# A selective-scan block on one core: softplus with two fitted factors, and five instead of four products with B per unit made by GpSimd

## The reference, cut to what matters

```
u = silu(causal_conv(in_proj(seq)))
dt, B, C = split(x_proj(u))
dt = softplus(dt_proj(dt) + bias)          # max(v, 0) + log(1 + exp(-|v|))
for each token t:
    h = exp(dt_t * A) * h + (dt_t * u_t) * B_t      # 256 channels x 16 states
    y_t = sum over states of h * C_t
out = out_proj((y + u * D) * silu(z))
```

## Time and profile before

| what | value |
|---|---|
| median of 3 runs | 1283.58 us |
| the profiled execution | 1284.42 us, its span 1282.6 us |
| instructions with a busy time | PE 3642, DVE 1341, ACT 1532, POOL 747 |
| chain that ended last, by engine | POOL 27%, DVE 24%, issue 21%, PE 19%, ACT 7% |
| mean granted TensorE clock | 0.936 of full speed |
| data moved | 116.78 MB, 90 GB/s over the span |

### The profile page before, as it was taken

One profiled execution on the slowest core, in us unless ns is written; L12 is line 12 of the kernel. 1 busy time (PEld: TensorE's weight loads), 2 busy tenths in 40 slices (PEclk: granted clock), 3 DMA queues, 4 the chain that ended last, 5 costly groups with the idle time before them and its releaser, 6 DMA issues.

```text
span 1282.6 us, 13041 instructions
## 1 busy us (share of the span) xinstructions
PE 1072.5 (84%) x3642; PEld 613.6 (48%) x3642; DVE 1150.1 (90%) x1341; ACT 819.0 (64%) x1532; POOL 1106.9 (86%) x747
## 2 busy tenths in 40 slices
PE   5678878888888887888888889888878878888797
PEld 4334545545545544544455455445445445454344
DVE  1299999999999999999999999999999999999782
ACT  2476766766666667757667666666667676576543
POOL 4199898898898898998988988988988989989663
PEclk8699998998998999999999989989999999998898
DMA  6222221221222312212222212222122132222561
GB/s 162 76 76 76 81 100 65 98 100 58 99 76 86 101 57 105 100 57 98 87 77 80 101 57 99 93 71 99 59 102 101 57 105 100 74 99 87 181 206 37
DMA packets 64538, 116.78 MB, mean 91 GB/s; under 512 B 34218, under 2 KB 47954, under 8 KB 64466
## 3 DMA queue, kind: packets, MB, share of 16 engines
q1 hardware_dynamic: 64466, 115.96, 26.9%
HBM read 108.47 MB, written 7.47 MB: 90 GB/s over the span
## 4 chain that ended last, share of the span: by engine, by line
POOL 27%; DVE 24%; issue 21%; PE 19%; ACT 7%; POOLq 0%; DMA 0%; DVEq 0%; SPq 0%; ACTq 0%
POOL SCAN L414 15%; DVE SCAN L984 15%; PE Yp L711 7%; POOL SCAN L426 6%; DVE SCAN L939 5%; PE PP L740 2%; PE PP L862 2%; PE PP L790 2%; PE PP L842 2%; POOL XN L451 2%; PE PP L835 1%; DVE GATES L968 1%; ACT SGZ L599 1%; POOL GATES L419 1%; POOL XN L442 1%
## 5 line engine op out<-in xcount | busy, mean ns | idle before, releaser
L984 DVE TENSOR_TENSOR_SCAN SCAN<-DA,CAR,SCAN 128x384 f32<-128x384 f32 x768 | 729.8, 1000 | 39.3 <-POOL SCAN L426 35.7
L414 POOL TENSOR_TENSOR SCAN<-SCAN,CS 128x768 f32<-128x768 f32 x384 | 692.3, 1817 | 23.1 <-DVE SCAN L984 18.9
L711 PE MATMUL Yp<-SCAN,IDENT 128*128 128x384 f32 x1536 | 592.6, 511 | 101.1 <-POOL SCAN L414 93.0
L491 ACT ACTIVATE DA<-UDT,A 128x384 f32<-128x384 f32 x768 | 441.6, 581 | 365.3 <-DVE SCAN L984 362.5
L711 PEld LDWEIGHTS Yp<-SCAN,IDENT 128*128 128x128 f32 x1536 | 288.8, 198 | 309.8 <-POOL SCAN L414 147.3
L939 DVE TENSOR_TENSOR SCAN<-UDT,BB 128x768 f32<-128x768 f32 x288 | 268.4, 932 | 11.1 <-PE BB L693 9.2
L426 POOL TENSOR_TENSOR SCAN<-UDT,BS 128x768 f32<-128x768 f32 x96 | 174.4, 1817 | 0.0
L862 PE MATMUL PP<-XN,WT 128*128 128x384 f32 x384 | 140.4, 501 | 0.0
L446 POOL TENSOR_TENSOR UDT<-UDT 128x768 f32<-128x768 f32 x24 | 43.5, 1811 | 69.9 <-DVE UDT L1068 69.9
L862 PEld LDWEIGHTS PP<-XN,WT 128*128 128x128 f32 x384 | 75.6, 199 | 56.7 <-issue 11.7
L693 PE MATMUL BB<-PT,SEL 96*128 96x384 bf16 x288 | 97.7, 340 | 4.1 <-DVE SCAN L939 4.1
(11 more groups left out here) (167 smaller groups left out, 1090.2 us busy)
## 6 DMA issues: line engine op xcount, KB each, us to landing
CS<-bc_rows SPq DMA_DIRECT2D x96, 768.0 KB, 4.1
BS<-bc_rows SPq DMA_DIRECT2D x24, 768.0 KB, 6.0
out<-XN SPq DMA_DIRECT2D x32, 192.0 KB, 2.5
X<-in_x SPq DMA_DIRECT2D x24, 192.0 KB, 3.5
X<-in_L_ffn_memory_tokens SPq DMA_DIRECT2D x16, 256.0 KB, 3.0
XN<-in_L_ffn_memory_tokens SPq DMA_DIRECT2D x16, 256.0 KB, 3.3
bc_rows<-XDT SPq DMA_DIRECT2D x24, 48.0 KB, 1.5
X<-in_L_ffn_memory_router SPq DMA_DIRECT2D x1, 512.0 KB, 4.0
```

The source lines that it names most:

```text
L414: pool.tensor_tensor(M[:, n1 % MRING], HB[:, n1 % HRING], over_halves(CS[:, n1 % CRING]), ALU.mult).then_inc(m_ready, 1)
L491: act.activation(DA[:, h, 0:T], DT[:, par, h], ACT.Exp, scale=A[:, h, n:n + 1])\
L711: last = pe.matmul(Yp[:, h, 0:T], IDENT[:, :], M[:, n3 % MRING, h], start=n3 == 0, stop=n3 == NS - 1)
L984: dve.tensor_tensor_scan(HB[:, s % HRING, h], DA[:, h, 0:T], HB[:, s % HRING, h], CAR[:, ds(J * NS * HALVES + s * HALVES + h, 1)], ALU.mul ...
```

## The change

1. The approximation of log(1+e) is another product of fitted factors. ScalarE makes r = 1/(2 + e) as before (bias 2.0, no scale), then two independent squares of r with different biases in step 10 (into SS and SR). It squares SS once more in step 11 and SR once more in step 12. That is four squares, each with a bias, in place of two. GpSimd's product L431 is gone; the factor e enters in VectorE's first fused multiply.
2. VectorE's two fused multiplies and the last operation (now a subtraction, since the sign sits in a constant) move from step 13 to step 12: the first ahead of scan 12, the others behind it. GpSimd's L446 stays in step 13.
3. `POOL_STATES` gets state 11. GpSimd makes that product with B in step 9, VectorE does 11 instead of 12 per unit, TensorE spreads 11 rows. BS grows to five rows, 960 KB per unit.
4. `load_b` waits until all of the unit's products with B on GpSimd are made.
5. Two slots of BB are used by the running count of VectorE's products, not by the index in the unit, since 11 is odd.

```diff
-POOL_STATES = (3, 5, 7, 9)
+POOL_STATES = (3, 5, 7, 9, 11)
...
+    p = (1.28926229, 1.34076026, -1.527418, -0.43882777, 0.72873143, 0.06986066, 1.76617345)
+    k = p[0] * p[5] * p[6]
+    h1, h2 = 0.5 / p[5], 0.5 / p[6]
+    return p[1], k ** 0.5, h1, k * (h1 * h1 + p[2] / p[5]), p[3], h2, p[4] / p[6] - h2 * h2
+FIT_X, FIT_S, FIT_V, FIT_A, FIT_Z, FIT_W, FIT_B = fit_factors()
+FIT_BIAS = (2.0, FIT_X, -FIT_S * FIT_V, FIT_Z, FIT_W)
...
@@ sync: load_b @@
                 sp.wait_ge(rows_written, 16 * (unit + 1))
+                positive(sp, dbu_pool, NPOOL * unit)
...
@@ gpsimd @@
-                if front and s == 11:
-                    pool.wait_ge(sq_e_ready, f + 1)
-                    pool.tensor_tensor(SE[:, :, :], SE[:, :, :], SR[:, :, :], ALU.mult).then_inc(cr_ready, 1)
...
@@ scalar @@
+                if front and s == 11:
+                    act.wait_ge(fac_chain, 3 * f + 2)
+                    act.activation(SS[:, :, :], SS[:, :, :], ACT.Square, bias=FITB[:, 2:3], scale=FIT_S)\
+                        .then_inc(fac1_ready, 1)
                 if front and s == 12:
-                    act.wait_ge(cr_ready, f + 1)
-                    act.activation(SR[:, :, :], SE[:, :, :], ACT.Square, scale=1.0 / LOG_C).then_inc(r2_ready, 1)
-                    act.wait_ge(r2_ready, 2 * f + 1)
-                    act.activation(SS[:, :, :], SR[:, :, :], ACT.Square, bias=LOGB[:, 1:2]).then_inc(r2_ready, 1)
+                    act.wait_ge(fac_chain, 3 * f + 3)
+                    act.activation(SR[:, :, :], SR[:, :, :], ACT.Square, bias=FITB[:, 4:5]).then_inc(fac2_ready, 1)
...
-                    act.activation(SR[:, :, :], SE[:, :, :], ACT.Ln, bias=LOGB[:, 0:1], scale=1.0 / LOG_C)\
-                        .then_inc(sp_chain, 1)
+                    act.activation(SR[:, :, :], SE[:, :, :], ACT.Ln, bias=FITB[:, 0:1]).then_inc(sp_chain, 1)
                 if front and s == 10:
                     act.wait_ge(sp_chain, 3 * f + 3)
-                    act.activation(SR[:, :, :], SR[:, :, :], ACT.Exp, scale=-1.0).then_inc(sq_e_ready, 1)
+                    act.activation(SR[:, :, :], SR[:, :, :], ACT.Exp, scale=-1.0).then_inc(fac_chain, 1)
+                    act.wait_ge(fac_chain, 3 * f + 1)
+                    act.activation(SS[:, :, :], SR[:, :, :], ACT.Square, bias=FITB[:, 1:2]).then_inc(fac_chain, 1)
+                    act.activation(SR[:, :, :], SR[:, :, :], ACT.Square, bias=FITB[:, 3:4]).then_inc(fac_chain, 1)
...
@@ tensor: spread_b @@
-                pe.matmul(BB[:, dve_index(n) % 2, 0:T], SEL[:, n], PT[:, par], start=True, stop=True)\
+                pe.matmul(BB[:, before % 2, 0:T], SEL[:, n], PT[:, par], start=True, stop=True)\
...
@@ vector: drive @@
-                dve.tensor_tensor(HB[:, n % HRING], DTU[:, par], over_halves(BB[:, dve_index(n) % 2, 0:T]), ALU.mult)\
+                dve.tensor_tensor(HB[:, n % HRING], DTU[:, par], over_halves(BB[:, (NDVE * unit + dve_index(n)) % 2, 0:T]), ALU.mult)\
...
@@ vector: step, ahead of the scan @@
-                if front and s == 13:
-                    dve.wait_ge(r2_ready, 2 * f + 1)
-                    dve.scalar_tensor_tensor(out=SE[:, :, :], in0=SR[:, :, :], scalar=LOG_D, in1=SE[:, :, :],
+                if front and s == 12:
+                    dve.wait_ge(fac1_ready, f + 1)
+                    dve.scalar_tensor_tensor(out=SE[:, :, :], in0=SS[:, :, :], scalar=-FIT_A, in1=SE[:, :, :],
                                              op0=ALU.add, op1=ALU.mult).then_inc(m1_done, 1)
...
@@ vector: step, behind the scan @@
-                if front and s == 13:
-                    dve.wait_ge(r2_ready, 2 * f + 2)
+                if front and s == 12:
+                    dve.wait_ge(fac2_ready, f + 1)
                     dve.wait_ge(m1_done, 2 * f + 1)
-                    dve.scalar_tensor_tensor(out=SE[:, :, :], in0=SS[:, :, :], scalar=LOG_H, in1=SE[:, :, :],
+                    dve.scalar_tensor_tensor(out=SE[:, :, :], in0=SR[:, :, :], scalar=FIT_B, in1=SE[:, :, :],
                                              op0=ALU.add, op1=ALU.mult).then_inc(m1_done, 1)
                     dve.wait_ge(relu_done, f + 1)
                     dve.wait_ge(m1_done, 2 * f + 2)
-                    dve.tensor_tensor(DT[:, fp], DT[:, fp], SE[:, :, :], ALU.add).then_inc(dt_ready, 1)
+                    dve.tensor_tensor(DT[:, fp], DT[:, fp], SE[:, :, :], ALU.subtract).then_inc(dt_ready, 1)
```

More of the change, by code:

```diff
@@ L39, with fit_factors @@
 LOG_C, LOG_D, LOG_G, LOG_H = 0.34222454, 1.83313539, 0.33814541, 1.75319741 ** 2
-POOL_STATES = (3, 5, 7, 9)
+def fit_factors():
+    p = (1.28926229, 1.34076026, -1.527418, -0.43882777, 0.72873143, 0.06986066, 1.76617345)
[5 more added lines that the diff above has]
+POOL_STATES = (3, 5, 7, 9, 11)
 NPOOL = len(POOL_STATES)
@@ L110, in build @@
         EPSC = sb("EPSC", [P, 1]); EPST = sb("EPST", [P, 1])
-        LOGB = sb("LOGB", [P, 2])
+        LOGB = sb("LOGB", [P, 2]); FITB = sb("FITB", [P, len(FIT_BIAS)])
         WNAT = SCAN[:, 0:512].rearrange("p (k c) -> p k c", k=4)
@@ L167, in build @@
         parts_ready = sem("parts_ready"); dtp_ready = sem("dtp_ready"); sp_chain = sem("sp_chain")
-        relu_done = sem("relu_done"); sq_e_ready = sem("sq_e_ready"); cr_ready = sem("cr_ready"); r2_ready = sem("r2_ready"); m1_done = sem("m1_done"); dt_ready = sem("dt_ready"); dtu_ready = sem("dtu_ready")
+        relu_done = sem("relu_done"); fac_chain = sem("fac_chain"); fac1_ready = sem("fac1_ready"); fac2_ready = sem("fac2_ready"); m1_done = sem("m1_done"); dt_ready = sem("dt_ready"); dtu_ready = sem("dtu_ready")
         b_ready = sem("b_ready"); dbu_dve = sem("dbu_dve"); dbu_pool = sem("dbu_pool")
@@ L376, in _ @@
             pool.memset(LOGB[:, 1:2], -LOG_G).then_inc(const_ready, 1)
+            for i, v in enumerate(FIT_BIAS):
+                pool.memset(FITB[:, i:i + 1], v).then_inc(const_ready, 1)
             pool.wait_ge(zeroed, 2)
@@ L462, in _ @@
             act.preload_act_table_set("natural_log_exp_and_others")
-            act.wait_ge(const_ready, 7)
+            act.wait_ge(const_ready, 7 + len(FIT_BIAS))
             def weights():
```

## The result

The change makes the kernel slower: 1304.03 us (median of 4 runs, 1302.98 to 1305.45) against 1285.12 us for the kernel before beside it (4 runs), a ratio of 1.0149 with an interval of 1.0129 to 1.0170. The prediction was 1271, with a range of 1250 to 1288. The profiled execution took 1304.52 us (span 1302.7), 20.1 us more than the profiled 1284.42 of before.

A forecast was written before the change was run, and what follows sets the result against it. A loop through GpSimd (31.46 us) and VectorE (18.11) was taken to bound the 49.67 us unit. 23 intervals x 0.48 = 11.0 us plus 1.5 at the start made 12.5 us, giving 1271 us, range 1250 to 1288.

The forecast's parts named there:

- GpSimd runs about 1 us ahead: At state 9: GpSimd's part, 31.5 us, is shorter than VectorE's 32.53, so its state-11 C product starts at 636.6.
- Scan 10 moves from 632.45 to 632.0: Behind scan 9: VectorE loses the state-11 product, 0.93 us, but TensorE's sums limit the gain to 0.45 us.
- The break-even: End of the sum for DT after scan 9: no change at 17.14 us; the forecast itself had 16.66.
- VectorE's stretch from DT to scan 9: VectorE's work from the sum for DT to scan 9: 29.84 us, now 32.53 with 2.69 moved behind the sum.
- The kind of collision: The three two-input operations around scan 12: each waits for one GpSimd operation at most and ends 0.82 us later.
- The vanishing waits for products with B: In front of scans 3, 5 and 9: VectorE's waits for GpSimd, 1.74 us a unit, should vanish.
- Scan 11 that doesn't wait for its product: GpSimd's state-11 product ends at 634.1, scan 11 can start at 634.7: no wait, 0.6 us to spare, cost 0.
- The larger load: The five-row B load takes 7.5 us and lands by about 642, before its first user at 645: cost 0.
- The third: Rival: queued GpSimd operations pass waiting VectorE operations; DT 17.72 us after scan 9, unit 50.25, 1295 us; chance 0.15.
- The second: Rival: no change, because the sum for DT ends about 0.5 us later than forecast; 1277 to 1290 us; chance 0.20.
- The start: Unit before the first main one: a GpSimd product of 1.8 us gives way to a Square of 0.84; gain 1.5 us.
- The end: The last unit has no softplus and its end goes by other work: 0.

The follow-up runs named there:

- e1: The changed kernel with the two fused multiplies and the subtraction for DT back in step 13: 1286.37 us.
- e2: The changed kernel with four products with B on GpSimd, state 11 back on VectorE: 1293.74 us.
- e4: The changed kernel with one SBUF operand of each of the three VectorE operations replaced by DA in PSUM, so its output is not the reference's: 1276.60 us.
- e5: The changed kernel with GpSimd's normalization of unit J+3 moved from step 15 to step 13, behind DT * U: 1296.21 us.
- e3: The kernel before with only the fifth product with B given to GpSimd, softplus as before: 1337.68 us.
- e12: The changed kernel with three softplus squares behind the first normalization's square in the unit before the first main one: 1302.78 us.
- e13: The changed kernel with the three operations in step 13, squares of steps 11 and 12 behind their decays, four GpSimd products with B: 1287.74 us.
- e7: The kernel before with GpSimd's normalization of unit J+3 moved from step 15 to step 13, ahead of DT * U: 1267.84 us.

## Why the prediction was wrong, point by point

**The step that failed.** "GpSimd runs about 1 us ahead of where it was at state 9, which is why I let its state-11 product start at 636.6 above and not at 637.6." It doesn't run ahead. The prediction compared GpSimd's old 31.5 us with VectorE's new 32.53 and kept the first as it was, but the same edit that put 2.69 us behind the sum for DT, scan 13 among it, also gave GpSimd a new wait: its first product with C behind L456 needs scan 13. In after that is the 0.89 us at 658.31, and GpSimd's stretch from L456 to the end of its product for state 9 is 32.38 us (605.48 to 637.86) instead of 31.46. Both engines arrive together; scan 9 even waits 0.33 us.

A second term was mis-sized, "Scan 10 moves from 632.45 to 632.0, a gain of 0.45." It was 3.61 us after scan 9 before and is 3.52 now, a gain of 0.09: TensorE's sums for L979 end about 3.0 us after scan 9, not 2.62, and L979 waits 0.34 us for them. In e1, where scan 9 waits 0.72 us for its product as before, scan 10 does start 3.09 us after it. The forecast had counted on both, the gain and the vanished wait.

So scan 11 ends 8.12 us after scan 9 and not 7.7, and a product with C that starts right behind it can't end at 9.6 in any case; in e2, where it does start there, it ends at 10.1. By these figures about 0.5 us of the delay at this product belong to the missing gain and the handover, and another 0.5 to GpSimd's missing lead (an estimate).

From scan 9 on, six GpSimd operations of 1.78 us follow without a gap, and the product with C for state 11 ends 10.62 us after scan 9 (648.51), not 9.6. Scan 11 was done in time (646.01). Everything behind it moves with it: first multiply 11.43 for 10.46, second 15.97 for 14.9, DT 17.65 for 16.66. With DT to scan 9 at 32.48 the unit is 50.13. The break-even that the prediction named, 17.14, lies between. That the place of the three operations costs the time is shown (e1 takes 17.7 us off), and so are the collisions there (e4, 27.4) and the fifth product's share (e2, 10.3); these overlap and don't add. That the lead alone would have brought the gain is not: e5 took the 0.89 us gap away and got 7.8 us.

**What came as forecast.** VectorE's stretch from DT to scan 9 (32.53 forecast, 32.48 measured). The kind of collision: each of the three operations ends 0.8 us behind one GpSimd operation, and without the three the unit is 1.27 us shorter (e4) for a forecast 1.44. Their lengths were 1.95, 2.45 and 1.57 us, where the forecast had 1.3, 1.75 and 1.65. The vanishing waits for products with B (1.74 to 0.31 us a unit). Scan 11 that doesn't wait for its product. The larger load stayed hidden; the page has it at 5.3 us, less than the 6.0 of the smaller one before and than the forecast's 7.5.

**The rivals.** The third had the right sign and, with 17.72 and 50.25 us, nearly the measured 17.65 and 50.13, but not by its mechanism, so that is luck: no queued operation passed a waiting one in the unit shown, each lost just the one that ran. In one unit of after out of the 24 the first multiply was passed by one operation (2.66 us, at 1148.67). The mechanism exists, as e3 shows, but isn't what made this change slower. The second had the break-even right and a chance of 0.20 where it was the forecast's weakest joint: the margin was 0.48 us and one GpSimd wait of 0.89 us is more than that.

The Trainium skill, page "SBUF — State Buffer", section "Summary: rules for kernel authors", says that when a VectorE operation has two SBUF inputs and the GpSimd operation reads SBUF, the second one to issue blocks fully until the first finishes. e1, e4 and after agree (beside GpSimd 0.95 us without a second SBUF input, 1.6 to 2.5 with). e3 goes beyond it: there the blocked operation was asked before three others began, and they still went first.

**The sum.** Forecast -12.5 us, measured +20.1. Of these 32.6 us, 22 intervals that are 0.58 us longer instead of 0.48 shorter make 23.4. The start was to gain 2.0 (1.5 and one interval) and lost 2.54: 4.5. The end was to cost nothing and costs 4.65.

**The start.** It was priced by the softplus alone. The gain forecast there did come: from the Exp that begins the softplus to the first product DT * U it takes 8.66 us (49.77 to 58.43) instead of 10.38, and 1 to 2 us were forecast. But the square of the normalization behind it on ScalarE was late, and with it TensorE's spread of B: the first product with B starts at 63.97 instead of 61.10.

```profile
54.14 0.92 ACT L527 ACTIVATE GATES<-GATES,FITB 128x768 f32<-128x768 f32 x1
54.96 0.51 ACT L657 ACTIVATE SQ<-XC 128x384 f32<-128x384 f32 x1
```

```profile
63.97 1.82 DVE L954 TENSOR_TENSOR SCAN<-UDT,BB 128x768 f32<-128x768 f32 x2 [2.41 <-PE BB L708]
```

**The end.** It was priced at nothing, although the 2.69 us that the forecast put behind the sum for DT stand behind the last one too. In before and in all seven kernels with the three operations in step 13 the first scan of the last unit starts 6.16 us behind the last product DT * U. In after, e2, e5 and e12 it is 11.0 us, in e4 11.4. Behind that product now stand scan 13 and the product for state 14, and with them small operations of the routing that before stood ahead of it. Two of these lie beside GpSimd work and take 1.82 and 0.94 us, before 0.22 and 0.18. So these 4.85 us belong to the placement.

From that scan to the end it takes 83.7 us in after and 83.9 before. That stretch differs between kernels by more than the placement explains (e1 82.4, e13 86.2, e7 87.1, all with the operations in step 13), and its cause stays open. Within it the first routed sum on TensorE takes 10.15 us at a granted clock of 0.70, before 8.63 (from 1203.67) at 0.82, but that is made good again by the end. The rows of after, with the first scan of the last unit, and the stretch of the routed sum:

```profile
1209.96 1.82 DVE L1059 TENSOR_SCALAR SQ<-SQ 4x8 f32<-4x8 f32 x1
1211.81 0.94 DVE L1061 TENSOR_TENSOR SQ<-IDENT,SQ 4x32 f32<-4x32 f32 x1
...
1219.01 1.91 DVE L999 TENSOR_TENSOR_SCAN SCAN<-DA,CAR,SCAN 128x384 f32<-128x384 f32 x2
```

```profile
1223.95:1234.10 10.15, 10.15 (x17) 4.30 (x18) 1.93 (x2) 4.60 (x13) 6.67 (x4) 0.70 0.58 187
```
